# Attention side jobs of a transformer block, cut into two 64-row halves and put among the score tiles, with a new timetable

## The chip, the cores and the metric

The kernel runs on one core of a Trainium2 chip. The metric is the time of one execution on the device in microseconds (us), as the median of several runs; beside it stands one profiled execution, whose trace every row below comes from. The engines are named as in the profile: PE is TensorE's matmul, PEld its weight load, DVE is VectorE, ACT is ScalarE, POOL is GpSimd, SP is SyncE (SPq its queue of DMA issues).

## The reference

Input x is 8 batches of 1024 tokens of 256 numbers. Two stages follow, each with a layer norm before it, a layer norm on its result and the input added:

```
x = x + layernorm(attention(layernorm(x)))      # 16 heads of 16, softmax over 1024 keys, biases on q, k, v, out
x = x + layernorm(experts(layernorm(x)))        # 16 experts (8 chosen per token) and one shared, hidden size 128
```

Only the attention stage is touched by the change.

## The kernel before, in words

**Units.** In the attention stage a batch has 8 steps (four heads and one half of the 512 queries each), and a step has 8 units (one chunk of 128 keys each). So there are 64 units u in a batch and 512 in all. A unit works on four score tiles (128 keys x 512 queries, one per head). For each unit PE issues

- `st`: four score tiles (L535). A head's q and k lie in a 64-row stack, rows 0 to 63 or 64 to 127, so that a tile is a matmul with K=64, and two with different rows can run beside each other. ACT takes the exponential of each (L925) into `probs`. The tiles have three banks: tile n waits for the exponential of tile n-3.
- `smax`: four matmuls of the same size (L547), two steps ahead of the tiles, with queries and keys exchanged. DVE takes the row maxima of each (L1036). They too have three banks: the n-th waits until DVE has read the one three before it.
- `pv`: probs times v for the four heads (L557), eight matmul instructions of 128 rows x 32 columns. It waits for all four exponentials of its unit, and at the first unit of a step until ACT has copied `o_bank` away (L833, `o_stored`).
- in some units a part of a side job, all of them in one bank, `job_bank`.

In `batch` the order on PE in unit u is: two tiles of the next unit, one maximum matmul, pv, a maximum, a tile, a maximum, a tile, the job part, a maximum. So between one pv and the next there are four tiles and four maximum matmuls: at pv of unit u the tiles up to 4u+5 have been issued.

**Side jobs.** The table `JOBS` gives the unit of each: XT transposes the next batch's normed x (L573), QK (L581) and V (L590) project it, OP (L602) is the output projection of the batch before, SH (L594) transposes the row maxima of a step for its shift. A QK or V or OP job is six or twelve matmuls with K=128, cut into two parts for two units. A job's result is read at the start of the unit after its last part: `if u - 1 in JOBS`. DVE reads QK (L1057), XT (L1053) and SH (L1069) ahead of that unit's four maxima (at the first unit of a step `combine_maxima`, L1043, stands before both); QK and XT are first read by ACT, after the four exponentials of that unit; V and OP are read by ACT alone. The next job may not write `job_bank` before that (list `before`).

**The row for the shift.** The tiles of a step need the maxima of that step in row 32 of their stacks: SH, then DVE (L1069), then four DMAs of `load_shift` (L352). The first tile of a step waits for them (`shift_loaded`). All DMAs of the stage are issued by SP, in an order written out by hand. In its middle stand, for batch b:

```
gather(b, 3)
load_shift(b, 5)
...
if not last:
    load_stack(b + 1, 0, False)
gather(b, 4)
load_shift(b, 6)
```

`load_stack(b + 1, 0)` waits until DVE has read the fourth QK job of batch b + 1, then issues 14 DMAs (L339, L343). `gather` issues eight (L363, L364).

**Last batch.** From unit 50 on no maxima are left; the tiles have six banks (`late`), and all four tiles of the next unit are issued before pv.

Of the kernel before, what the change touches and what calls it, by code (L numbers as in the profile page):

```python
# [5 lines left out]
BATCHES, SEQ, D = 8, 1024, 256  # L6
HEADS = 16
DH = D // HEADS
CH = 128
# [7 lines left out]
RING = 3  # L17
VW = 2 * DH
EXPERTS, HID, TOPK = 16, 128, 8
ALL_E = EXPERTS + 1  # L20
# [25 lines left out]
for _kind, _off, _i, _at in (  # L46
# [3 lines left out]
    for _n, _u in enumerate(_at):  # L50
        JOBS[_u] = (_kind, _off, _i + _n // 2, _n % 2)

# [12 lines left out]
def skipped(job, first, last):  # L65
    kind, off, i, part = job
    return off == -1 and first or off == 1 and last or last and kind == "SH" and i == STEPS


# [7 lines left out]
def both_stages(nc, x, x1, wq, wk, wv, wo, biases, ob, ident_dram, out, comb_dram, gate_w, w_gate, w_up, w_down,  # L77
# [8 lines left out]
    with ctx:  # L86
# [126 lines left out]
        exp_done = sem("exp_done")  # L213
        pv_done = sem("pv_done")
        smax_ready = sem("smax_ready")
        smax_read = sem("smax_read")
# [302 lines left out]
        def _(pe):  # L519
            mm = nc.tensor.matmul  # L520
            before = []

            def st(U, s, kc, j, new_step):

                q, f, p, e, tile = s // 2, s % 2, j // 2, j % 2, 4 * U + j
                if new_step is not None:
                    pe.wait_ge(shift_loaded, 64 * (new_step + 1))
# [10 lines left out]
            def smax(S, s, kc, half, e):  # L538

                q, f = s // 2, s % 2  # L540
                p, c = kc // HC, kc % HC
                tok = f * HALF + c * CH
                n = 32 * S + 4 * kc + 2 * half + e
                if n >= RING:
                    pe.wait_ge(smax_read, n - RING + 1)
                rows = slice(64 * e, 64 * e + 64)
                mm(sm_bank[n % RING][:, :], q_stack[q][p][rows, tok:tok + CH],  # L547
                   k_stack[q][p][rows, half * HALF:(half + 1) * HALF], start=True, stop=True).then_inc(smax_ready, 1)

            def pv(U, S, s, kc):  # L550

                q = s // 2
                if kc == 0 and not (isinstance(S, int) and S == 0):
                    pe.wait_ge(o_stored, S)
                pe.wait_ge(exp_done, 4 * U + 4)
                for j in range(4):
                    last = mm(o_bank[32 * j:32 * j + 32, :], v_quad[q][:, kc, VW * j:VW * j + 32],  # L557
                              probs[0 if kc % 2 == 0 else 1][:, j, :], start=(kc == 0), stop=(kc == CHUNKS - 1))
                last.then_inc(pv_done, 1)


            def job(kind, B, i, part=None, job_bank=job_bank, banks=1, before=before):
# [41 lines left out]
                if part != 0:  # L604
                    last.then_inc(job_ready[kind], 1)


            READ = {"XT": "xT_read", "LG": "lg_read", "CB": "cbT_read", "GT": "gT_read"}
# [90 lines left out]
            for S in range(2):  # L699
                for n in range(4 * CHUNKS):  # L700
                    smax(S, S, n // 4, n // 2 % 2, n % 2)
# [5 lines left out]
            for j in range(RING):  # L707
                st(0, 0, 0, j, 0)

            def batch(b, first, last):  # L710
                for u in range(UNITS):
# [8 lines left out]

                    def maximum(half, e):
                        if maxima:
                            smax(S + 2, (s + 2) % STEPS, kc, half, e)

                    def scores(j):
                        if u + 1 < UNITS:
                            st(U + 1, (u + 1) // CHUNKS, (u + 1) % CHUNKS, j, S + 1 if kc == CHUNKS - 1 else None)
                        elif not last:
                            st(U + 1, 0, 0, j, S + 1)

                    if u == 0 and first:
                        st(U, s, kc, 3, None)
                    late = last and u >= 50
                    scores(0)
                    scores(1)
                    if late:
                        scores(2)
                        scores(3)
                    maximum(0, 0)
                    if last and u == UNITS - 1:  # L740
                        gu(0, 0, 0, True)
                    pv(U, S, s, kc)
                    maximum(0, 1)
                    if not late:
                        scores(2)
                    maximum(1, 0)
                    if not late:
                        scores(3)
# [42 lines left out]
        def _(act):  # L791
# [122 lines left out]
            def batch(b, first, last):  # L914
                for u in range(UNITS):
                    s, kc = u // CHUNKS, u % CHUNKS
                    U, S = UNITS * b + u, STEPS * b + s
                    for j in range(4):
# [4 lines left out]
                        if j == 0 and U >= 2:  # L923
                            act.wait_ge(pv_done, U - 1)
                        nc.scalar.activation(probs[kc % 2][:, j, :], bank_of(4 * U + j)[:, :],  # L925
                                             ACT.Exp).then_inc(exp_done, 1)
# [61 lines left out]
        def _(dve):  # L988
# [39 lines left out]

            def reduce(S, s, kc, half):

                f = s % 2
                p, c = kc // HC, kc % HC
                for e in range(2):
                    n = 32 * S + 4 * kc + 2 * half + e
                    dve.wait_ge(smax_ready, n + 1)
# [254 lines left out]
            for S in range(2):  # L1290
                for kc in range(CHUNKS):
                    reduce(S, S, kc, 0)
                    reduce(S, S, kc, 1)
                if S == 0:
                    combine_maxima(0, 0)
                    job("SH", 0, 0)

            def batch(b, first, last):
                for u in range(UNITS):
# [9 lines left out]
                    if maxima:  # L1309
                        reduce(S + 2, (s + 2) % STEPS, kc, 0)  # L1310
                    if u in SPLITS and not (first and SPLITS[u][0]):
# [15 lines left out]
                    if maxima:  # L1327
                        reduce(S + 2, (s + 2) % STEPS, kc, 1)
                    if not last and u in X_STATS:
# [263 lines left out]
```

## Time and profile before

| | us |
|---|---|
| median of 3 runs | 2856.01 (2855.09 to 2858.19) |
| the profiled execution's own time | 2851.14 |
| its span, first to last instruction | 2849.4 |
| PE busy | 2746.2 (96%) |
| DVE busy | 2233.9 (78%) |
| ACT busy | 1632.6 (57%) |
| mean granted TensorE clock | 0.989 of full speed |

The attention stage takes the first 57% of the span, the experts the rest. In the attention stage PE and DVE are both nearly full, in the expert stage only PE is. Busy shares of PE are no measure of how near it is to its peak, since a matmul's record begins when it is issued to the array and overlaps with the next one.

### The profile page before, as it was taken

To read this page: it belongs to the slowest core of one execution; us is meant where nothing else is said; L and a number is where in the kernel's file an instruction comes from. 1 tells how busy PE (TensorE), PEld (TensorE's weight loads), DVE (VectorE), ACT (ScalarE), POOL (GpSimd) and SP (SyncE) were. 2 spreads that over 40 slices of the span, in tenths; PEclk is the share of its full clock that TensorE was granted. 3 is DMA by queue.
4 is the path that set the end of the run, shared out by engine and by line. 5 is a ranking of instruction groups with operands and counts; after the bars stand their busy time and mean duration, and the time that the engine had idled before them with its cause. 6 is when DMAs were issued, how large, how long until landed. Compare 5 with 4: busy or idle time off the path is not lost.

```text
span 2849.4 us, 47584 instructions
## 1 busy us (share of the span) xinstructions
PE 2746.2 (96%) x16514; PEld 1685.8 (59%) x16514; DVE 2233.9 (78%) x4679; ACT 1632.6 (57%) x3095; POOL 954.7 (34%) x997
## 2 busy tenths in 40 slices
PE   5999999999999999999999999999999999999997
PEld 3434333343343343333433388888888888888886
DVE  4898998999999999999999667666666666666654
ACT  1477777777777777777778843333333333333332
POOL 4041462543533624625435545111111111111112
PEclk8899999999999999999999999999999999999999
DMA  5313422343234134333432323222222222232221
GB/s 88 55 27 57 65 60 54 57 85 57 56 63 64 42 65 64 64 56 59 69 64 72 88 78 105 82 79 77 73 82 83 79 79 71 83 82 79 79 74 54
DMA packets 136639, 197.32 MB, mean 69 GB/s; under 512 B 22336, under 2 KB 84816, under 8 KB 134352
## 3 DMA queue, kind: packets, MB, share of 16 engines
q1 hardware_dynamic: 136400, 194.29, 30.6%
q8 instruction: 131, 2.15, 0.3%
q14 instruction: 108, 0.88, 0.1%
HBM read 108.74 MB, written 17.30 MB: 44 GB/s over the span
## 4 chain that ended last, share of the span: by engine, by line
PE 82%; SPq 6%; DVE 5%; ACT 4%; issue 2%; POOL 1%; DMA 1%; POOLq 0%; ACTq 0%; DVEq 0%
PE o_bank L557 14%; PE y_bank L680 13%; PE g_bank L666 13%; PE u_bank L666 13%; PE sm_bank L547 12%; PE st_bank L535 7%; PE job_bank L581 4%; SPq L339 3%; DVE score_max L1036 3%; ACT probs L925 3%; PE job_bank L590 2%; PE job_bank L602 1%; SPq L352 1%; SPq L363 1%; SPq L364 1%
## 5 line engine op out<-in xcount | busy, mean ns | idle before, releaser
L1036 DVE TENSOR_REDUCE score_max<-sm_bank 128x1 f32<-128x512 f32 x2048 | 1302.3, 681 | 114.4 <-PE sm_bank L547 110.7
L925 ACT ACTIVATE probs<-st_bank 128x512 f32<-128x512 f32 x2023 | 1077.8, 601 | 319.0 <-PE st_bank L535 316.5
L547 PE MATMUL sm_bank<-qk_stack 64*128 64x512 f32 x2048 | 804.3, 465 | 18.7 <-DMA qk_stack<-qk_stack 10.5
L535 PE MATMUL st_bank<-qk_stack 64*128 64x512 f32 x2023 | 753.3, 453 | 30.1 <-ACT probs L925 24.5
L547 PEld LDWEIGHTS sm_bank<-qk_stack 64*128 64x128 f32 x2048 | 332.5, 187 | 581.6 <-DVE score_max L1036 537.9
L557 PE MATMUL o_bank<-probs,v_quad 128*32 128x512 f32 x4096 | 545.5, 605 | 9.1 <-ACT o_sb L833 7.0
L1193 DVE TENSOR_TENSOR h<-gate_act,u_bank 128x512 f32<-128x512 f32 x256 | 176.2, 688 | 312.9 <-ACT gate_act L887 312.9
L887 ACT ACTIVATE gate_act<-g_bank 128x512 f32<-128x512 f32 x272 | 162.4, 597 | 418.1 <-PE u_bank L666 418.0
L535 PEld LDWEIGHTS st_bank<-qk_stack 64*128 64x128 f32 x2023 | 313.7, 184 | 99.6 <-ACT probs L925 74.6
L898 ACT ACTIVATE h_hi<-h 128x512 fp32r<-128x512 f32 x272 | 172.2, 633 | 325.5 <-DVE h L1196 287.8
L680 PE MATMUL y_bank<-f_w_hi,h_hi 128*128 128x256 f32 x1088 | 311.7, 286 | 0.1
L680 PE MATMUL y_bank<-f_w_lo,h_hi 128*128 128x256 f32 x1088 | 307.6, 283 | 0.0
L680 PE MATMUL y_bank<-f_w_hi,h_lo 128*128 128x256 f32 x1088 | 307.6, 283 | 0.0
L1473 POOL TENSOR_SCALAR f_x_in<-f_x_in,f_mv,f_rstd 128x256 f32<-128x256 f32 x64 | 90.3, 1419 | 624.8 <-DVE f_rstd L1107 624.8
L1437 POOL TENSOR_TENSOR recip_tmp<-sum_part,recip 128x512 f32<-128x512 f32 x96 | 123.7, 1289 | 466.6 <-DVE recip L1077 461.6
L1204 DVE TENSOR_TENSOR h_lo<-h,h_hi 128x512 fp32r<-128x512 f32 x272 | 189.4, 696 | 47.2 <-ACT h_hi L898 43.6
L666 PE MATMUL g_bank<-f_xT_hi,f_w_hi 128*128 128x512 f32 x544 | 215.4, 396 | 0.5 <-DVE h L1193 0.5
L666 PE MATMUL g_bank<-f_xT_lo,f_w_hi 128*128 128x512 f32 x544 | 215.0, 395 | 0.0
L680 PEld LDWEIGHTS y_bank<-f_w_hi,h_hi 128*128 128x128 f32 x1088 | 207.5, 191 | 8.6 <-DVE h_lo L1204 0.3
L680 PEld LDWEIGHTS y_bank<-f_w_hi,h_lo 128*128 128x128 f32 x1088 | 207.8, 191 | 8.0
L666 PE MATMUL u_bank<-f_xT_hi,f_w_lo 128*128 128x512 f32 x544 | 211.9, 389 | 0.0
L666 PE MATMUL g_bank<-f_xT_hi,f_w_lo 128*128 128x512 f32 x544 | 211.6, 389 | 0.0
(200 smaller groups left out, 3874.5 us busy)
## 6 DMA issues: line engine op xcount, KB each, us to landing
cb<-comb_dram SPq DMA_DIRECT2D x256, 256.0 KB, 3.6
qk_stack<-qk_parts SPq DMA_DIRECT2D x360, 128.0 KB
x_in<-in_x SPq DMA_DIRECT2D x8, 1024.0 KB, 6.6
o_part<-o_sb SPq DMA_DIRECT2D x256, 32.0 KB, 2.0
sum_part<-o_sb SPq DMA_DIRECT2D x256, 32.0 KB, 2.0
x_res<-in_x SPq DMA_DIRECT2D x16, 512.0 KB, 3.9
x<-x_res SPq DMA_DIRECT2D x16, 512.0 KB, 3.1
f_x_in<-x SPq DMA_DIRECT2D x16, 512.0 KB, 3.9
```

The source lines that it names most:

```text
L535: mm(bank_of(tile)[:, :], k_stack[q][p][rows, kc * CH:(kc + 1) * CH], q_stack[q][p][rows, f * HALF:(f + 1) * HALF], start=True, stop=True) ...
L547: mm(sm_bank[n % RING][:, :], q_stack[q][p][rows, tok:tok + CH], k_stack[q][p][rows, half * HALF:(half + 1) * HALF], start=True, stop=True ...
L557: last = mm(o_bank[32 * j:32 * j + 32, :], v_quad[q][:, kc, VW * j:VW * j + 32], probs[0 if kc % 2 == 0 else 1][:, j, :], start=(kc == 0), ...
L666: last = mm(bank[:, :], w_exp[b][:, e, col + k * HID:col + (k + 1) * HID], fxT[par][a][:, k, :], start=(t == 0), stop=(t == len(steps) - 1))
L680: last = mm(y_bank[:, c, :], h[i][a][:, c * CH:(c + 1) * CH], w_exp[b][:, e, 2 * D:3 * D], start=(e == 0 and t == 0 and c % 2 == 0), stop= ...
L887: a_(gate_act[i][:, :], g_bank[i][:, :], ACT.Silu).then_inc(E["silu_done"], 1)
L898: a_(h[i][0][:, :], h32[i][:, :], ACT.Copy).then_inc(E["h_hi_done"], 1)
L925: nc.scalar.activation(probs[kc % 2][:, j, :], bank_of(4 * U + j)[:, :], ACT.Exp).then_inc(exp_done, 1)
L1036: v.reduce_max(score_max[f][:, HC * (2 * p + e) + c, half:half + 1], sm_bank[n % RING][:, :], AX_X).then_inc(smax_read, 1)
L1193: v.tensor_tensor(h32[i][:, :], gate_act[i][:, :], u_bank[i][:, :], ALU.mult).then_inc(E["gated_done"], 1)
L1204: v.tensor_tensor(h[i][1][:, :], h32[i][:, :], h[i][0][:, :].bitcast(F32), ALU.subtract).then_inc(E["h_ready"], 1)
L1437: g.tensor_tensor(recip_tmp[:, :], sum_part[f][:, :], recip[:, :], ALU.mult).then_inc(recip_chain, 1)
```

## The change

- XT, QK, V and OP jobs are issued by a new function `job_rows`: their K=128 matmuls become two halves with K=64 (rows 0 to 63 first, then rows 64 to 127), each half in three thirds. A unit's job part is thus six pieces. They stand between the tiles and the maximum matmuls, each next to one of the other rows. The second half waits for the first (`job_rows_done`), and so does the second part for the first part.
- In every unit pv now comes first, then tile 4u+6, a maximum, tile 4u+7, two maxima, tile 4u+8, a maximum, tile 4u+9. In a unit with a job part the first piece stands ahead of tile 4u+6 and the second ahead of the first maximum.
- The heads are taken in the order 0, 2, 1, 3 (`HEAD_AT`), and the maxima in an order of rows that depends on whether the unit has a job (`MAX_AT`).
- New timetable: XT at units 22, 24, 26, 28 (before 23, 24, 27, 28); QK at 30, 33, 36, 39 and 52, 55, 58, 61, each with the unit after it (before 29, 31, 35, 37 and 51, 53, 55, 59); V at 42, 44, 47, 50 (before 39, 43, 45, 47); SH at 32 in place of 33, else as before; OP as before.
- The special order of the last batch's units from 50 on is gone (the six banks are still there). Six tiles are issued ahead of the first unit instead of three.

```diff
-JOBS = {
-    23: ("XT", 1, 0, None), 24: ("XT", 1, 1, None), 27: ("XT", 1, 2, None), 28: ("XT", 1, 3, None),
-}
-for _s in range(STEPS):
-    JOBS[8 * _s + 1] = ("SH", 0, _s + 1, None)
+JOBS = {}
+for _i, _u in enumerate((1, 9, 17, 25, 32, 41, 49, 57)):
+    JOBS[_u] = ("SH", 0, _i + 1, None)
+for _i, _u in enumerate((22, 24, 26, 28)):
+    JOBS[_u] = ("XT", 1, _i, None)
 for _kind, _off, _i, _at in (
-        ("OP", -1, 0, (5, 6, 7, 8)), ("OP", -1, 2, (15, 16, 20, 21)),
-        ("QK", 1, 0, (29, 30, 31, 32, 35, 36, 37, 38)), ("V", 1, 0, (39, 40, 43, 44, 45, 46, 47, 48)),
-        ("QK", 1, 4, (51, 52, 53, 54, 55, 56, 59, 60))):
+        ("OP", -1, 0, (5, 7)), ("OP", -1, 2, (15, 20)), ("QK", 1, 0, (30, 33, 36, 39)),
+        ("V", 1, 0, (42, 44, 47, 50)), ("QK", 1, 4, (52, 55, 58, 61))):
...
+            def job_rows(job, b, e, third):
...
+                rows = slice(64 * e, 64 * e + 64)
+                if third == 0:
+                    if e == 1 or part == 1:
+                        pe.wait_ge(job_rows_done, rows_done[0])
+                    if e == 0 and part != 1:
+                        if before:
+                            pe.wait_ge(*before.pop(0))
...
+                elif kind == "QK":
+                    m, half, n = i // 4, i // 2 % 2, "qk"[i % 2]
+                    a, w = PARTS[third]
+                    last = mm(job_bank[:, :], w_parts[n][w][rows, part, m * 128:(m + 1) * 128],
+                              xT[a][rows, part, half * HALF:(half + 1) * HALF],
+                              start=(part == 0 and third == 0 and e == 0), stop=(part == 1 and third == 2 and e == 1))
+                else:
...
+                    for k in range(KD):
+                        last = mm(job_bank[:, part * D:(part + 1) * D], left[a][rows, k, c * CH:(c + 1) * CH],
+                                  right[w][rows, k, :], start=(e == 0 and third == 0 and k == 0),
+                                  stop=(e == 1 and third == 2 and k == KD - 1))
...
                     pv(U, S, s, kc)
-                    maximum(0, 1)
-                    if not late:
-                        scores(2)
-                    maximum(1, 0)
-                    if not late:
-                        scores(3)
-                    if u in JOBS and not skipped(JOBS[u], first, last):
-                        kind, off, i, part = JOBS[u]
-                        job(kind, b + off, i, part)
-                    maximum(1, 1)
+                    if with_job:
+
+                        job_rows(JOBS[u], b, 0, 0)
+                        st(4 * U + 6)
+                        job_rows(JOBS[u], b, 0, 1)
+                        maximum(0)
+                        job_rows(JOBS[u], b, 0, 2)
+                        st(4 * U + 7)
+                        maximum(1)
+                        maximum(2)
+                        st(4 * U + 8)
+                        job_rows(JOBS[u], b, 1, 0)
+                        maximum(3)
+                        job_rows(JOBS[u], b, 1, 1)
+                        st(4 * U + 9)
+                        job_rows(JOBS[u], b, 1, 2)
+                    else:
+                        st(4 * U + 6)
+                        maximum(0)
+                        st(4 * U + 7)
+                        maximum(1)
+                        maximum(2)
+                        st(4 * U + 8)
+                        if u in JOBS and not skipped(JOBS[u], first, last):
+                            job("SH", b, JOBS[u][2])
+                        maximum(3)
+                        st(4 * U + 9)
```

## Rows read from the trace of the kernel before

**Rows 1.** Six whole batches in one window: length, busy and count per engine, clock, DMA

```profile
294.74:1463.13 1168.39, 1140.52 (x7152) 460.00 (x7152) 1091.51 (x1999) 914.08 (x1729) 521.12 (x613) 1.00 0.34 60
```

**Rows 2.** Timeline of PE, a unit without a job: start, us, line, matmul, count

```profile
740.81 1.06 PE L557 MATMUL o_bank<-probs,v_quad 128*32 128x512 f32 x8
741.81 0.49 PE L547 MATMUL sm_bank<-qk_stack 64*128 64x512 f32 x1
...
742.15 0.62 PE L547 MATMUL sm_bank<-qk_stack 64*128 64x512 f32 x2
742.39 0.39 PE L535 MATMUL st_bank<-qk_stack 64*128 64x512 f32 x1
...
743.09 0.50 PE L547 MATMUL sm_bank<-qk_stack 64*128 64x512 f32 x1
743.51 1.07 PE L557 MATMUL o_bank<-probs,v_quad 128*32 128x512 f32 x8
```

**Rows 3.** Timeline of DVE and of ACT in the same unit

```profile
742.34 2.48 DVE L1036 TENSOR_REDUCE score_max<-sm_bank 128x1 f32<-128x512 f32 x4 [0.22 <-PE sm_bank L547]
...
742.37 2.06 ACT L925 ACTIVATE probs<-st_bank 128x512 f32<-128x512 f32 x4 [0.90 <-PE st_bank L535]
```

**Rows 4.** Timeline of PE, a unit with a QK job part

```profile
792.23 1.06 PE L557 MATMUL o_bank<-probs,v_quad 128*32 128x512 f32 x8
793.22 0.49 PE L547 MATMUL sm_bank<-qk_stack 64*128 64x512 f32 x1
...
793.88 0.50 PE L581 MATMUL job_bank<-xT_hi,wq_hi 128*128 128x512 f32 x1
794.22 0.40 PE L581 MATMUL job_bank<-xT_lo,wq_hi 128*128 128x512 f32 x1
...
794.77 0.49 PE L547 MATMUL sm_bank<-qk_stack 64*128 64x512 f32 x1
...
795.44 0.64 PE L557 MATMUL o_bank<-probs,v_quad 128*32 128x512 f32 x4
```

**Rows 5.** Timeline of PE, the V job part of another unit

```profile
822.21 0.28 PE L590 MATMUL job_bank<-wv_hi,xT_lo 128*128 128x256 f32 x1
822.33 0.28 PE L590 MATMUL job_bank<-wv_lo,xT_hi 128*128 128x256 f32 x1
```

**Rows 6.** Timeline of PE, first and last pv record of a unit with an XT job

```profile
755.90 1.07 PE L557 MATMUL o_bank<-probs,v_quad 128*32 128x512 f32 x8 [0.21 <-ACT o_sb L833]
...
758.82 0.64 PE L557 MATMUL o_bank<-probs,v_quad 128*32 128x512 f32 x4
```

**Rows 7.** Timeline, PE and DVE: unit 33, which reads a QK job and has SH

```profile
783.33 1.06 PE L557 MATMUL o_bank<-probs,v_quad 128*32 128x512 f32 x8
...
786.30 0.64 PE L557 MATMUL o_bank<-probs,v_quad 128*32 128x512 f32 x4
...
783.90 0.72 DVE L1057 SCALAR_TENSOR_TENSOR qk_parts<-job_bank,bias,qk_parts 128x512 fp32r<-128x512 f32 x1
784.53 2.47 DVE L1036 TENSOR_REDUCE score_max<-sm_bank 128x1 f32<-128x512 f32 x4
786.92 0.27 DVE L1069 TENSOR_SCALAR shift_row<-job_bank 16x128 fp32r<-16x128 f32 x1
```

**Rows 8.** Timeline of SP's queue, units 39 to 45, and PE's first tile of step 6

```profile
803.18 10.90 SPq L339 DMA_DIRECT2D qk_stack<-qk_parts  x12
...
820.62 2.53 SPq L352 DMA_DIRECT2D qk_stack<-shift_row  x4
...
826.12 0.72 PE L535 MATMUL st_bank<-qk_stack 64*128 64x512 f32 x2
```

**Rows 9.** Timeline of SP's queue and of PE in unit 14

```profile
724.41 2.54 SPq L352 DMA_DIRECT2D qk_stack<-shift_row  x4
...
728.03 0.56 PE L535 MATMUL st_bank<-qk_stack 64*128 64x512 f32 x2 [1.06 <-DMA qk_stack<-shift_row]
```

**Rows 10.** Timeline of PE, a late unit (57) of the last batch

```profile
1628.51 1.06 PE L557 MATMUL o_bank<-probs,v_quad 128*32 128x512 f32 x8 [0.36 <-ACT probs L925]
...
1630.47 1.06 PE L557 MATMUL o_bank<-probs,v_quad 128*32 128x512 f32 x8 [0.23 <-ACT probs L925]
```

More of the change, by code:

```diff
@@ L18 @@
 VW = 2 * DH
+HEAD_AT = (0, 2, 1, 3)
+MAX_AT = {True: ((0, 1), (0, 0), (1, 1), (1, 0)), False: ((0, 0), (1, 0), (0, 1), (1, 1))}
 EXPERTS, HID, TOPK = 16, 128, 8
@@ L36 @@
 PARTS = [(0, 0), (1, 0), (0, 1)]
-JOBS = {
-    23: ("XT", 1, 0, None), 24: ("XT", 1, 1, None), 27: ("XT", 1, 2, None), 28: ("XT", 1, 3, None),
-}
-for _s in range(STEPS):
-    JOBS[8 * _s + 1] = ("SH", 0, _s + 1, None)
+JOBS = {}
[3 more added lines that the diff above has]
+    JOBS[_u] = ("XT", 1, _i, None)
 for _kind, _off, _i, _at in (
[3 rows of a table removed]
+        ("OP", -1, 0, (5, 7)), ("OP", -1, 2, (15, 20)), ("QK", 1, 0, (30, 33, 36, 39)),
+        ("V", 1, 0, (42, 44, 47, 50)), ("QK", 1, 4, (52, 55, 58, 61))):
     for _n, _u in enumerate(_at):
-        JOBS[_u] = (_kind, _off, _i + _n // 2, _n % 2)
+        for _part in range(2):
+            JOBS[_u + _part] = (_kind, _off, _i + _n, _part)
 X_STATS = {0: 0, 2: 1, 5: 2, 6: 3, 7: 4, 8: 5, 9: 6, 10: 7}
@@ L67, in skipped, with among_scores @@
     return off == -1 and first or off == 1 and last or last and kind == "SH" and i == STEPS
+def among_scores(u, first, last):
+    return u in JOBS and JOBS[u][0] != "SH" and not skipped(JOBS[u], first, last)
 def wait_apart(engine, semaphore, value, passed):
@@ L521, in _, with st @@
             before = []
[L523 to L527, printed above, removed]
+            def st(tile):
+                U, i = tile // 4, tile % 4
+                if U >= UNITS * BATCHES:
+                    return
+                S, kc, j = U // CHUNKS, U % CHUNKS, HEAD_AT[i]
+                s = S % STEPS
+                q, f, p, e = s // 2, s % 2, j // 2, j % 2
+                if kc == 0 and i == 0:
+                    pe.wait_ge(shift_loaded, 64 * (S + 1))
                 if tile >= LATE + 6:
@@ L536, in st, with smax @@
                    q_stack[q][p][rows, f * HALF:(f + 1) * HALF], start=True, stop=True).then_inc(st_ready, 1)
-            def smax(S, s, kc, half, e):
+            def smax(S, s, kc, i, with_job):
                 q, f = s // 2, s % 2
                 p, c = kc // HC, kc % HC
+                half, e = MAX_AT[with_job][i]
                 tok = f * HALF + c * CH
-                n = 32 * S + 4 * kc + 2 * half + e
+                n = 32 * S + 4 * kc + i
                 if n >= RING:
@@ L552, in pv @@
                 q = s // 2
-                if kc == 0 and not (isinstance(S, int) and S == 0):
+                if kc == 0 and S > 0:
                     pe.wait_ge(o_stored, S)
@@ L706, in _ @@
             before.pop(0)
-            for j in range(RING):
-                st(0, 0, 0, j, 0)
+            for tile in range(6):
+                st(tile)
             def batch(b, first, last):
@@ L719, in batch, with maximum @@
                         pe.wait_ge(v_copied, QUADS * b + s // 2 + 1)
-                    def maximum(half, e):
+                    with_job = among_scores(u, first, last)
+                    def maximum(i):
                         if maxima:
[L723 to L736, printed above, removed]
-                        scores(2)
-                        scores(3)
-                    maximum(0, 0)
+                            smax(S + 2, (s + 2) % STEPS, kc, i, with_job)
                     if last and u == UNITS - 1:
@@ L1027, in seed_a, with reduce @@
                 seed(seed_no(f"a{f}", B), var_a[f][:, :], mv_a[f][:, :, 1], rstd_a[f][:, :])
-            def reduce(S, s, kc, half):
+            def reduce(S, s, kc, pair, with_job):
                 f = s % 2
                 p, c = kc // HC, kc % HC
-                for e in range(2):
-                    n = 32 * S + 4 * kc + 2 * half + e
+                for i in (2 * pair, 2 * pair + 1):
+                    half, e = MAX_AT[with_job][i]
+                    n = 32 * S + 4 * kc + i
                     dve.wait_ge(smax_ready, n + 1)
@@ L1291, in _ @@
                 for kc in range(CHUNKS):
-                    reduce(S, S, kc, 0)
-                    reduce(S, S, kc, 1)
+                    reduce(S, S, kc, 0, False)
+                    reduce(S, S, kc, 1, False)
                 if S == 0:
@@ L1309, in batch @@
                     if maxima:
-                        reduce(S + 2, (s + 2) % STEPS, kc, 0)
+                        reduce(S + 2, (s + 2) % STEPS, kc, 0, among_scores(u, first, last))
                     if u in SPLITS and not (first and SPLITS[u][0]):
@@ L1327, in batch @@
                     if maxima:
-                        reduce(S + 2, (s + 2) % STEPS, kc, 1)
+                        reduce(S + 2, (s + 2) % STEPS, kc, 1, among_scores(u, first, last))
                     if not last and u in X_STATS:
```

34 lines of the change are left out of this document (30 added, 4 removed).

## The prediction

> **What bounds the kernel now.** I read the window over six whole batches first. It gives 1168.39/6 = 194.73 us a batch, 3.04 a unit, with PE 98% and DVE 93% busy at the full clock [rows 1]. The clock has nothing to give, so the question is what ends a unit. That is read from the timelines, as the distance from one pv to the next.
>
> A unit without a job takes 2.70 us [rows 2]. Its PE steps are: pv to the first pair of score matmuls 1.00, first to second pair 0.34, second to third 0.24. The reader should see that the fourth maximum matmul comes only at 743.09, behind a gap. It waits for the first of the four reduces, which began 0.53 after its matmul and takes about 0.68 (2.48 for four, 0.60 apart) [rows 3]: 742.34 + 0.68 + 0.06 = 743.08. ACT gives the same end: 742.37, one exponential later (the four take 2.06, so about 0.49 apart) and 0.60 long, is 743.46, and pv starts at 743.51. So 2.70 is a round trip PE to DVE or ACT and back; neither engine is full. Since the second matmul of a pair starts with the first, I call both by one time.
>
> A unit with a QK part takes 3.21 [rows 4]. Here PE sets the end: 0.99, then 0.66 to the job, 0.34 and 0.24 between its matmuls, 0.31 back to 64 rows, 0.67 to pv. Each change of tiling costs: 0.31 to 0.34 where 0.24 is the step inside one. That is the 36 units of 64 which the change attacks.
>
> **The change part by part.** All times from here are after the start of the unit's pv.
>
> *A QK unit.* Seven pairs stand in one tiling: job and tile 6, job and maximum 0, job and tile 7, maxima 1 and 2, tile 8 and job, maximum 3 and job, tile 9 and job. By PE's steps they start at 1.00, 1.34, 1.58, 1.82, 2.06, 2.30, 2.54, and pv follows 0.33 later: 2.87. The columns streamed are the same as before; two changes of tiling are saved. But maximum 0 is now in the second pair, at 1.34 and not at 1.00, and all four maxima lie behind the pv. DVE can start at 1.34 + 0.43 = 1.77 (a matmul whose load is hidden lasts 0.39, not 0.50), ends at 2.45, and maximum 3, in the same one of three banks, goes at 2.51 instead of 2.30. Its weight load carries the wait, so the next of its rows follows after 0.34: 2.85, and pv at 3.18. I take 3.17 against 3.21: 16 units a batch, -0.6. The low end is PE's own 2.87, the high one 3.37, if every pair takes 0.34.
>
> The step of 0.24 inside 64 rows is seen once per plain unit [rows 2]. The Trainium skill, TensorE: Matmul & The Clock Gate, Part 3, The mechanism, says that a weight load overlaps with a running matmul only when the row group differs. In a run of pairs that use both row groups each load would then stand open, 0.34 a pair; the trace has 742.15 to 742.39 with the same two row groups in both pairs, so here it does not agree. By the rule a QK unit is 3.37, by the row 3.17.
>
> *V and OP units.* Each piece is two matmuls of 256 columns, 0.12 apart [rows 5]. Matmuls start in order, so tile 6 and maximum 0 come 0.12 later: 3.29. Against about 3.21 that is +0.08: V 8 x 0.08 = +0.6 a batch. OP counts only at 15, 16, 20, 21, because unit 14 waits for DMAs anyway (below): 4 x 0.08 = +0.3.
>
> *XT units.* They took 2.92 [rows 6]: four short transposes. In the new order maximum 0 stands behind three of them (at about 1.40) and the same round trip gives 3.23: 4 x 0.31 = +1.2.
>
> *The units that read a job.* QK and XT are read by DVE ahead of the four maxima of the next unit, 0.63 from its start to the next reduce [rows 7]. Before, this mostly fell into a job unit, where DVE had slack; four times it fell into a plain unit, and unit 33 took 2.97 [rows 7]. Now all twelve reads fall into plain units. After a QK unit DVE is free at 1.77 + 4 x 0.60 - 3.17 = 1.00, reads until 1.63, and maximum 0 is reduced from 1.63, not 1.53: +0.10 each, +1.2, with 0.2 for unit 32, which has `combine_maxima` too, less four times 0.2 before: +0.6.
>
> *SH next to a job.* The first piece of a job now stands right behind pv, and it waits until `job_bank` has been read. The timetable puts a job directly behind SH five times: units 26, 33, 42, 50, 58; before there was always a unit between. SH is read by DVE after all four reduces of the unit before: the last one lets go at 744.73, which is 1.22 after pv [rows 3], the read takes 0.27 [rows 7], so the job starts at 1.55, not 1.00. Tile 6, and behind it ACT, and all of PE wait with it: 4 x 0.55. In unit 33 it is worse: unit 32 has combine (0.17), the QK read and a norm's statistics on DVE, and SH is read at 2.0, +1.0. Sum +3.2. Below: 0, if the read slipped into an earlier gap, which DVE's order excludes.
>
> *SP's queue.* This is the largest term. The fourth QK job moves from units 37, 38 to 39, 40. `load_stack` of the next batch waits for its read, and it stands ahead of `gather` 4 and `load_shift` 6, which the first tile of step 6 needs. From the first stack DMA to the last shift DMA it is 803.18 to 822.6, and from there to a tile that waits for it 1.65 (726.4 to 728.03 [rows 9]): 21.1 us at least [rows 8], up to 22.5 in other batches, 21.8 in the mean. The tile came at 826.12, so the slack was about 2 here and 1.1 in the mean. In the new order the DMAs can start at 1.75 in unit 41, and the tile is due at 1.58 in unit 46: 2.80 + 3.84 + 3 x 3.29 - 1.75 + 1.58 = 16.3. PE waits 21.8 - 16.3 = 5.5; of this 0.8 comes back because the exponentials for the next pv are done meanwhile: +4.7 a batch. Late next: `load_stack` 1, `gather` 5 and `load_shift` 7 behind it, 22 us more, against 25 to their tile, so nothing. Between 3 and 6 is my bound.
>
> Unit 14 is already such a wait: PE idles 1.06 before the tile [rows 9]. What is lost or won in units 0 to 13 of a batch is therefore mostly hidden, OP at 5 to 8 among it.
>
> *The last batch.* Without the special order tiles 6 and 7 of a unit come behind the pv again, and a late unit is a round trip of 2.70 and not 1.96 [rows 10]. Some ten units of 1.96 to 2.25 lose 0.6 each, about 1 comes back where the shift of step 7 is late anyway: +5. With the six early tiles, +0.
>
> *Nothing for* the head order and `MAX_AT`: pairs of opposite rows formed before too, and a plain unit keeps its round trip through ACT. The expert stage is the same.
>
> **Sum.** XT, QK and V for the next batch run in seven batches: 7 x (-0.6 + 0.6 + 1.2 + 0.6 + 3.2 + 4.7) = 68. OP 7 x 0.3 = 2, last batch 5: 75. The profiled execution's own time of 2851.1 becomes 2926. The median of the runs lies 4.9 above that execution, so I predict 2931, 2.6% slower.
>
> **The rivals.**
>
> *A, SP's queue is not late* (its DMAs go out faster when PE is slower to use them). For: 1.1 us of slack was there. Against: the chain is fixed issue time, 0.6 to 0.7 a DMA. Then 7 x 4.7 = 33 less: 2898.
>
> *B, the other side: the pieces cost PE nothing.* They would fill the time in which PE waits for DVE and ACT, and a job unit would be a plain one, 2.70: 252 job units x 0.47 = 118 less, of which some 30 go again to unit 14 and to a longer wait in 46: 2843, 0.4% faster. For: the gap ahead of 743.09 in a plain unit. Against: seven pairs at 0.24 make 2.87. It decides from about 2.76 a job unit downwards; maximum 0 would have to be free of its place in the second pair.
>
> *C, open weight loads:* seven pairs at 0.34, 0.20 more in 252 units, 50 us: 2981. The skill's rule above is this case. For: the step after every change of tiling is 0.34. Against: the 0.24 of the third pair.
>
> *D, a piece and its tile don't run beside each other.* Two more slots of 0.24 a unit at least, 0.5 x 252 = 126: 3057. For: the trace has no job in 64 rows. Against: tile and maximum matmul of the same shape do.
>
> **How the numbers follow.** Chances: the forecast 0.60 (its own range 2900 to 2960), A 0.13, B 0.10, C 0.10, D 0.07. The range from 2862 to 2980 leaves out B nearly whole, D, and the upper part of C, some 2 in 10. A change within 0.2% is about what a measurement of this kernel can't tell from none. Faster by more comes only from B: 0.09. Within 0.2%: 0.04, out of B and the edge of A. Slower: 0.87.
>
> **What would show it.** In the profile after: QK units at 3.17, V and OP 3.29, XT 3.23; step 0.24 between pairs inside a job unit; the fourth maximum matmul waiting for DVE in them. In the waits: PE for the shift's DMAs some 5 us in each of seven batches, at the first tile of step 6; PE's job matmuls waiting for L1069 five times a batch. A batch of about 205 us. The expert stage unchanged. I would be wrong if job units fell under 2.9, or if the tile of step 6 found its shift there.

## The result, and the profile after

| | before | after |
|---|---|---|
| median | 2857.1 us (2855.09 to 2859.19) | 2957.17 us (2953.89 to 2960.86) |
| span of the profiled execution | 2849.4 | 2954.3 |
| mean granted TensorE clock | 0.989 | 0.977 |

The ratio is 1.0352, 95% interval 1.034 to 1.0365: slower by 100 us, where 75 were forecast. The profiled executions took 2851.1 and 2956.1, 105 apart: that of the kernel before lies 6 under its median. The sums over units below are of these two.

The window over six whole batches, to be read against [rows 1] (length, then busy and count of PE, PEld, DVE, ACT, POOL, clock, DMA):

```profile
306.57:1553.34 1246.77, 1155.83 (x8112) 541.70 (x8113) 1082.41 (x2000) 907.96 (x1729) 524.73 (x613) 0.98 0.32 57
```

A batch takes 207.8 us, 13.1 more. PE is 93% busy where it was 98%, at a clock of 0.98 where it was 1.00. DVE and ACT do the same number of instructions in no more time (1082 and 908 us against 1092 and 914); PE has 960 more matmuls, halves of former ones, and is busy for 15 of the 78 us that six batches grew by. The other 63 are idle time of PE.

A unit with a QK part (unit 36), PE's timeline, against [rows 4]:

```profile
833.74 1.07 PE L573 MATMUL o_bank<-probs,v_quad 128*32 128x512 f32 x8
834.73 0.49 PE L657 MATMUL job_bank<-xT_hi,wq_hi 64*128 64x512 f32 x1
834.74 0.49 PE L550 MATMUL st_bank<-qk_stack 64*128 64x512 f32 x1
...
835.07 0.39 PE L563 MATMUL sm_bank<-qk_stack 64*128 64x512 f32 x1
835.29 0.39 PE L550 MATMUL st_bank<-qk_stack 64*128 64x512 f32 x1
...
835.52 0.40 PE L563 MATMUL sm_bank<-qk_stack 64*128 64x512 f32 x2
835.75 0.49 PE L657 MATMUL job_bank<-xT_hi,wq_hi 64*128 64x512 f32 x1
...
836.25 0.49 PE L563 MATMUL sm_bank<-qk_stack 64*128 64x512 f32 x1
...
836.58 0.39 PE L550 MATMUL st_bank<-qk_stack 64*128 64x512 f32 x1
...
836.91 0.64 PE L573 MATMUL o_bank<-probs,v_quad 128*32 128x512 f32 x4
```

The reader is to see job piece and tile starting together, steps of 0.22 to 0.24 between pairs inside the tiling, and one gap of 0.50 ahead of the fourth maximum matmul at 836.25. The unit takes 3.17, as forecast, against 3.21.

Unit 33, the job directly behind SH; PE's timeline:

```profile
823.57 1.07 PE L573 MATMUL o_bank<-probs,v_quad 128*32 128x512 f32 x8
825.52 0.50 PE L657 MATMUL job_bank<-xT_hi,wk_hi 64*128 64x512 f32 x1 [0.88 <-DVE shift_row L1141]
...
827.72 0.64 PE L573 MATMUL o_bank<-probs,v_quad 128*32 128x512 f32 x4
```

The first piece comes 1.95 after pv, not 1.00, and the unit takes 4.14.

SP's queue and PE in units 41 to 47 of the same batch, against [rows 8]; under it the window table of units 46, 47 and 48:

```profile
851.60 10.78 SPq L349 DMA_DIRECT2D qk_stack<-qk_parts  x12
...
869.52 2.54 SPq L362 DMA_DIRECT2D qk_stack<-shift_row  x4
...
873.14 0.79 PE L550 MATMUL st_bank<-qk_stack 64*128 64x512 f32 x1 [4.53 <-DMA qk_stack<-shift_row]
```

```profile
865.99:874.29 8.30, 3.38 (x19) 1.14 (x17) 4.00 (x7) 3.48 (x7) 0.00 (x0) 0.87 0.27 81
874.29:879.24 4.95, 4.95 (x30) 3.15 (x29) 2.07 (x4) 2.73 (x6) 0.00 (x0) 0.53 1.13 153
879.24:882.44 3.20, 3.20 (x31) 1.99 (x29) 2.50 (x6) 1.79 (x4) 0.00 (x0) 1.00 0.85 128
```

PE stands for 4.5 us, and then something the forecast did not have: the next unit, in which PE is never idle, takes 4.95 where its like takes 3.19. Its granted clock is 0.53, near the lower level of 1.2 GHz; one unit later it is 1.00 again.

Mean length of units over six batches, in us, from the distances between pv starts in the two traces (a table worked out, not a view; for XT the units before, then those after):

```
                              before  after           before  after
plain (0, 2, 13, 19)           2.70    2.74   unit 46    3.23    8.58
QK (30, 36, 37 ...)            3.22    3.18   unit 47    3.23    4.94
V (43, 44, 45 ...)             3.23    3.19   unit 26    2.71    3.65
XT (24, 27; 22, 24, 28)        2.91    3.17   unit 33    2.96    4.13
last batch, all               179.4   194.2   42, 50, 58 2.71    3.75, 3.64, 3.64
```

### The profile page after: what moved, and what is told of

Its sections match the earlier page's. It is cut to its first block, busy times and chain, and to the rows that moved or that the text cites. A ratio compares the mean times of both kernels' runs of the same rounds, so it can differ in the third digit from the quotient of the medians.

```text
span 2954.3 us, 49634 instructions
## 1 busy us (share of the span) xinstructions
PE 2766.5 (94%) x17634; PEld 1779.3 (60%) x17634; DVE 2222.5 (75%) x4679; ACT 1626.9 (55%) x3095; POOL 959.1 (32%) x997
## 4 chain that ended last, share of the span: by engine, by line
PE 66%; DVE 15%; SPq 11%; issue 4%; ACT 2%; DMA 1%; POOL 1%; POOLq 0%; ACTq 0%; DVEq 0%
PE y_bank L747 13%; PE g_bank L733 12%; PE u_bank L733 12%; DVE score_max L1108 12%; PE o_bank L573 10%; SPq L349 7%; PE sm_bank L563 6%; PE st_bank L550 5%; PE job_bank L657 3%; PE job_bank L665 2%; ACT probs L996 1%; SPq L362 1%; SPq L374 1%; SPq L353 1%; SPq L373 1%
## 5 line engine op out<-in xcount | busy, mean ns | idle before, releaser
L1108 DVE TENSOR_REDUCE score_max<-sm_bank 128x1 f32<-128x512 f32 x2048 | 1282.9, 680 | 221.5 <-PE sm_bank L563 216.7
L550 PE MATMUL st_bank<-qk_stack 64*128 64x512 f32 x2023 | 847.0, 451 | 42.7 <-DMA qk_stack<-shift_row 39.2
L563 PE MATMUL sm_bank<-qk_stack 64*128 64x512 f32 x2048 | 754.7, 456 | 61.9 <-DVE score_max L1108 43.4
L573 PE MATMUL o_bank<-probs,v_quad 128*32 128x512 f32 x4096 | 555.5, 615 | 20.7 <-ACT o_sb L904 11.6
L550 PEld LDWEIGHTS st_bank<-qk_stack 64*128 64x128 f32 x2023 | 363.2, 187 | 307.3 <-ACT probs L996 140.9
L563 PEld LDWEIGHTS sm_bank<-qk_stack 64*128 64x128 f32 x2048 | 344.9, 190 | 245.8 <-DVE score_max L1108 214.8
```

The source lines that it names most:

```text
L1108: v.reduce_max(score_max[f][:, HC * (2 * p + e) + c, half:half + 1], sm_bank[n % RING][:, :], AX_X).then_inc(smax_read, 1)
```

## The experiments

Every kernel here does the whole computation and leaves nothing out. "Before", run again beside them, had medians of 2854.4 to 2855.9; the ratios go by the one beside each. The changed kernel itself stands at 2957.17, ratio 1.0352.

**1. SP's order.** The changed kernel, with

```diff
-                if not last:
-                    load_stack(b + 1, 0, False)
                 gather(b, 4)
                 load_shift(b, 6)
+                if not last:
+                    load_stack(b + 1, 0, False)
```

> The changed kernel with one edit on SP: the stack load of the next batch is issued after gather 4 and the shift load of step 6, not before. Theory (SP's order makes the wait at unit 46, and the wait makes TensorE's clock fall in unit 47): units 46 and 47 go from 8.6 and 4.9 us to 2.74 and 3.19, a batch from 207.8 to about 200.2, the clock stays full, and the time falls by 7 x 7.6 = 53 us to about 2904. Rival (the issue time is only moved): the stack is then late for the first maximum of unit 48 or the shift of step 7 for unit 54, and at least half of the 7.6 us comes back there. Rival (the clock in 47 falls for another reason, such as the traffic of the stack's DMAs): 47 stays at 4.9, 12 us less gained.

Measured: 2907.62, ratio to before 1.0183 (1.0167 to 1.02). Units 46 and 47, the window table:

```profile
845.25:848.60 3.35, 2.95 (x18) 1.03 (x17) 2.65 (x5) 3.21 (x7) 0.00 (x0) 1.00 0.95 122
848.60:851.99 3.39, 3.27 (x30) 2.03 (x30) 3.26 (x6) 2.77 (x6) 0.00 (x0) 1.00 0.91 206
```

2904 was expected. A batch is 200.9, 6.9 less. The order of the DMAs was the wait, and with the wait gone the clock holds, although the stack's DMAs still run in these units (DMA share 0.95 and 0.91): the rival by which their traffic slows unit 47 falls. Unit 46 is 3.35 and not 2.74: there ACT reads the V job and makes a split, 1.25 us in all, ahead of the exponentials, and PE waits for an exponential:

```profile
847.14 0.49 PE L550 MATMUL st_bank<-qk_stack 64*128 64x512 f32 x1 [0.40 <-ACT probs L996]
```

**2. The table alone.** The kernel before, with nothing but the new `JOBS` (its code still puts a whole job between two maximum matmuls):

```diff
...
+for _i, _u in enumerate((1, 9, 17, 25, 32, 41, 49, 57)):
...
+for _i, _u in enumerate((22, 24, 26, 28)):
...
-        ("OP", -1, 0, (5, 6, 7, 8)), ("OP", -1, 2, (15, 16, 20, 21)),
-        ("QK", 1, 0, (29, 30, 31, 32, 35, 36, 37, 38)), ("V", 1, 0, (39, 40, 43, 44, 45, 46, 47, 48)),
-        ("QK", 1, 4, (51, 52, 53, 54, 55, 56, 59, 60))):
+        ("OP", -1, 0, (5, 7)), ("OP", -1, 2, (15, 20)), ("QK", 1, 0, (30, 33, 36, 39)),
+        ("V", 1, 0, (42, 44, 47, 50)), ("QK", 1, 4, (52, 55, 58, 61))):
...
```

> The kernel before with nothing but the new JOBS table: K=128 jobs, its own order on PE, its late order. Theory (the table alone makes SP late): the tile of step 6 is due in unit 46 at 16.1 us after the stack's DMAs can start, which need 21.8; with the lower clock after it some 7 us a batch, about 1 more for reads in plain units, none for SH since a job stands at the end of its unit: 2857 + 7 x 8 = 2913. Rival (the 64-row pieces and the order on PE cause most of it): under 2875.

Measured: 2915.83, ratio 1.0213 (1.019 to 1.0236). The same wait stands in the old code. Waits of one unit 46 (who waited for whom: us, times, longest), and units 46 and 47:

```profile
PEld st_bank L535 <- DMA qk_stack<-shift_row: 6.2, 1, 6.2
```

```profile
851.96:860.84 8.88, 3.10 (x18) 1.18 (x17) 3.71 (x6) 2.96 (x7) 0.00 (x0) 0.80 0.24 73
860.84:865.56 4.72, 4.72 (x24) 1.91 (x23) 2.11 (x4) 2.44 (x6) 0.00 (x0) 0.65 1.11 154
```

**3. The ring of three.** The changed kernel, in units with a job:

```diff
                         job_rows(JOBS[u], b, 0, 0)
-                        st(4 * U + 6)
-                        job_rows(JOBS[u], b, 0, 1)
                         maximum(0)
+                        job_rows(JOBS[u], b, 0, 1)
+                        st(4 * U + 6)
                         job_rows(JOBS[u], b, 0, 2)
```

> The changed kernel with maximum 0 and tile 4u+6 exchanged in units with a job, so that the maximum stands in the first pair. Theory (the ring of three maximum banks sets such a unit's 3.18): DVE starts 0.33 earlier, maximum 3 goes at 2.27 instead of 2.51, and the unit ends at 2.94, where the exponentials of tiles 6 and 7 come last: -0.24 in QK, V and XT units, some of it lost to units 14 and 46, so about 6 us a batch and 42 us in all: about 2914. Rival (PE's own steps or the pieces set the 3.18): no change, 2957. Rival (the tile put later costs as much as the maximum gains): within 10 us of 2957.

Measured: 2937.91, ratio 1.0289 (1.027 to 1.0309). The unit did what was expected: PE's timeline has pv at 826.63, the maximum at 1.00 after it, the fourth at 828.93 and the next pv at 829.59, 2.96 in all. The total gave 19 of the 43 us. The rest went to units 14 and 15, which grew from 3.30 and 3.38 to 4.87 and 4.50 (the DMAs of step 2 keep their time), in four batches of six with a low clock behind the wait, and to 46 (8.58 to 9.58). Unit 36, then units 14 and 15:

```profile
826.63 1.06 PE L573 MATMUL o_bank<-probs,v_quad 128*32 128x512 f32 x8
...
827.63 0.50 PE L563 MATMUL sm_bank<-qk_stack 64*128 64x512 f32 x1
...
828.93 0.49 PE L563 MATMUL sm_bank<-qk_stack 64*128 64x512 f32 x1
...
829.59 0.64 PE L573 MATMUL o_bank<-probs,v_quad 128*32 128x512 f32 x4
```

```profile
756.73:761.54 4.81, 2.61 (x18) 0.94 (x17) 3.60 (x8) 2.06 (x5) 0.00 (x0) 1.00 0.04 11
761.54:766.09 4.55, 4.46 (x30) 2.99 (x30) 2.38 (x6) 2.80 (x6) 0.00 (x0) 0.62 0.00 0
```

Here no DMA moved anything in unit 15 (last three columns: clock 0.62, DMA share 0.00, 0 GB/s), so the low clock follows PE's idle time, not traffic.

**4. The read of SH.** The changed kernel, on DVE (not in the last batch):

```diff
-                        if part != 0:
+                        if part != 0 and (kind != "SH" or last):
                             job(kind, b + off, i)
...
+                    if u in JOBS and JOBS[u][0] == "SH" and not last:
+                        job("SH", b, JOBS[u][2])
                     if maxima:
                         reduce(S + 2, (s + 2) % STEPS, kc, 1, among_scores(u, first, last))
```

> The changed kernel with DVE reading SH in its own unit, ahead of the last two maxima, instead of at the start of the next unit (not in the last batch). Theory (a job right behind SH waits for that read): units 26, 33, 42, 50 and 58 fall from 3.65, 4.13, 3.75, 3.64, 3.64 to 3.18; what 42 gives is lost at 46 where SP is late: 2.4 us a batch, 17 in all, about 2940. Rival (these units are long because of the transposes' or the read job's own place): they stay, and the read costs up to 0.2 in each SH unit: 2957 to 2970.

Measured: 2937.39, ratio 1.028 (1.026 to 1.0299). Units 26, 33, 42, 50, 58 became 3.18, 3.20, 3.19, 3.19, 3.17, together 2.9 a batch; unit 46 took 0.5 of it back (9.09), and unit 14 gave 0.5 (2.81).

**5. The late order.** Two tiles ahead of pv again from unit 50 of the last batch on:

```diff
+                    late = last and u >= 50
+                    if late:
+                        st(4 * U + 6)
+                        st(4 * U + 7)
...
                     else:
-                        st(4 * U + 6)
+                        if not late:
+                            st(4 * U + 6)
                         maximum(0)
-                        st(4 * U + 7)
+                        if not late:
+                            st(4 * U + 7)
```

> The changed kernel with the special order of the last batch's units from 50 on put back (two tiles ahead of pv). Theory (the round trip pv, tile, two exponentials, pv sets these units): units 51 to 61 go from 2.66 to about 2.05 as before, -0.6 in ten units: 5 to 6 us less, about 2951. Rival (the clock or the late shift sets the last batch's end): within 2 us of 2957.

Measured: 2952.92, ratio 1.0344 (1.033 to 1.0358). That is 4 less than the changed kernel, and the intervals of the two overlap, so the total alone decides little. In the trace six of the eleven units from 51 to 61 take 1.66 to 2.17 where most took 2.66, but units 49 and 50 grew from 4.07 and 3.83 to 4.98 and 5.20, both at a clock of 0.50 (see 10).

**6. Whole jobs, first try.** The six `job_rows` lines go out, and the job stands in one piece:

```diff
                         maximum(1)
+                        kind, off, i, part = JOBS[u]
+                        job(kind, b + off, i, part)
                         maximum(2)
```

> The changed kernel with its timetable and its order of tiles and maxima, but each job part issued whole with K=128 between the second and the third maximum. Theory (the two halves save 0.04 us a unit at their place and cost the wait for SH right behind pv): job units take 3.22, units 26, 33, 42, 50, 58 no more than that, the waits at 46 and 14 stay, so 2.9 less and 36 x 0.03 more a batch: about 2943, with up to 10 less where DVE's slack is used. Rival (the halves are worth the two changes of tiling, 0.35 a unit): 2957 + 252 x 0.35 - 20 = 3025.

Measured: 3034.35, ratio 1.063 (1.0616 to 1.0645), a miss by 91. The rival's 3025 is near, but by luck: its reason, that the halves save two changes of tiling worth 0.35 a unit, does not hold in number 8, where a whole job costs 0.04 a unit more. A job unit took 3.67. I had left the row order `MAX_AT` of the units with pieces: without the pieces between them three matmuls of rows 64 to 127 follow each other, and behind the job three of rows 0 to 63, and two more slots of 0.24 appear. Number 8 tests that.

**7. The table of before,** with the rest of the change: the diff of number 2 the other way round, on the changed kernel.

> The changed kernel with the JOBS table of before. Theory (the table is what makes SP late, but the first piece right behind pv needs the gaps of the new one): the wait at 46 shrinks from 5 to under 1, and in its place seven jobs a batch (units 24, 28, 31, 37, 39, 53, 55) stand directly behind a job that DVE reads, 0.7 us each: a batch of about 200, in all about 2905. Rival (the order on PE costs by itself what the table costs): 2950 or more. Rival (the table alone is the loss): under 2875.

Measured: 2931.85, ratio 1.0269 (1.0255 to 1.0283). The wait at 46 is gone as expected, but the jobs behind a job that DVE reads wait 1.0 us each and not 0.7, and they are eight, not seven (I had missed unit 29): 8.0 a batch against 4.9, so the total is 27 over the 2905 expected. PE in unit 31:

```profile
807.12 1.06 PE L573 MATMUL o_bank<-probs,v_quad 128*32 128x512 f32 x8
809.29 0.50 PE L657 MATMUL job_bank<-xT_hi,wk_hi 64*128 64x512 f32 x1 [1.11 <-DVE qk_parts L1129]
```

**8. Whole jobs, with rows in pairs.** Number 6, and the row order of a unit without pieces, on PE and in the reads on DVE:

```diff
-                            smax(S + 2, (s + 2) % STEPS, kc, i, with_job)
+                            smax(S + 2, (s + 2) % STEPS, kc, i, False)
...
-                        reduce(S + 2, (s + 2) % STEPS, kc, 0, among_scores(u, first, last))
+                        reduce(S + 2, (s + 2) % STEPS, kc, 0, False)
...
-                        reduce(S + 2, (s + 2) % STEPS, kc, 1, among_scores(u, first, last))
+                        reduce(S + 2, (s + 2) % STEPS, kc, 1, False)
```

> As e6_whole_jobs, but with the row order of the units without a job in all units, so that tiles and maxima stand in pairs of opposite rows. Theory (e6's 3.67 us were two more slots of 0.24 because three matmuls of one row group followed each other; a whole job at its own place takes 3.22): job units 3.22, XT 2.92, no wait behind SH at 26, 33, 42, 50, 58, waits at 14 and 46 as in the changed kernel: 2.4 us a batch less than it, about 2940. Rival (whole jobs between the maxima cost 3.67 whatever the rows): 3034 again.

Measured: 2936.81, ratio 1.029 (1.0276 to 1.0304). Job units 3.22, XT 2.91. So number 6 cost what it did by its rows, and at the place where the change puts them the 64-row halves lose 18 to 20 us against whole jobs. That is the wait behind SH: with it taken out (number 4, 2937.39) halves and whole jobs come out equal in the total.

**9. Before, with the new table and experiment 1's order:** the diffs of numbers 2 and 1, both on the kernel before.

> The kernel before with the new JOBS table and the SP order of e1_queue. Theory (SP's queue and the clock behind its wait are all that the table costs): against e2_timetable_alone units 46 to 48 lose 9 us a batch, which leaves about 196 a batch: 2866. Rival (the table costs something of its own, by DVE's reads in plain units): 2875 or more. Rival (the table is better once SP is out of the way): under 2852.

Measured: 2869.48, ratio 1.0053 (1.0039 to 1.0067). A batch is 196.3: of the table's loss of 61 us (number 2) 46 were SP's wait and the clock behind it.

**10. All repairs together.** The diffs of numbers 1, 3, 4 and 5, and one that takes 14 DMAs out of the way of unit 14:

```diff
-                    load_stack(b, 3, False)
                 for s in range(3):
...
                     load_shift(b, s + 2)
+                    if s == 0 and not first:
+                        load_stack(b, 3, False)
```

> The changed kernel with all repairs: maximum 0 in the first pair of a job unit, SH read in its own unit, the stack load of the next batch behind shift 6, the load of stack 3 behind shift 2, the late order of the last batch. Theory (each term is a wait of its own and they add): job units 2.95, no wait at 14, 26, 33, 42, 46, 50, 58, full clock: a batch of about 191.4 against 194.7 before, last batch under 179: about 2832, 0.8% faster than the kernel before. Rival (the time goes to a new wait, for DVE in the units that read a job or for SP's queue at steps 3 and 7): 2850 to 2870.

Measured: 2846.76, ratio 0.9971 (0.9962 to 0.998): faster than before by 0.3%, not by the 0.8% expected. A batch is 192.6, 1.2 more than expected. Against number 1 five units are 0.22 to 0.25 longer each, 15, 31, 39, 47 and 55, at whose end pv waits for the copy of `o_bank`, and unit 54 is 0.49 longer, because the first tile of step 7 now waits for its shift's DMAs: a part of the rival came true. The last batch is 187.0, more than before's 179.4. The wait at the first tile of step 7, then the last batch's units 47 to 50, window table:

```profile
842.89 0.50 PE L551 MATMUL st_bank<-qk_stack 64*128 64x512 f32 x1 [0.45 <-DMA qk_stack<-shift_row]
```

```profile
1587.20:1591.92 4.72, 3.14 (x19) 1.14 (x18) 4.72 (x10) 2.44 (x5) 4.72 (x4) 1.00 0.03 7
1591.92:1595.23 3.31, 3.05 (x14) 0.95 (x13) 1.46 (x2) 2.54 (x6) 1.34 (x1) 0.62 0.21 50
1595.23:1600.21 4.98, 4.98 (x16) 1.57 (x16) 1.34 (x8) 2.99 (x7) 0.00 (x0) 0.50 0.05 13
1600.21:1605.42 5.21, 5.21 (x18) 1.92 (x17) 1.23 (x6) 1.81 (x5) 0.00 (x0) 0.50 0.45 129
```

**11. The same with whole jobs:** number 10 with the diffs of numbers 6 and 8 in place of number 3's.

> As e10_best, but each job part whole with K=128 behind the second maximum, and the row order of plain units. Theory (once the ring of maximum banks is out of the way the 64-row halves are worth 3.22 - 2.95 = 0.27 in a job unit of QK, V and OP, less where pv waits for the copy of o_bank, and nothing in XT): about 6.5 us a batch more than e10_best: 2847 + 48 = 2895. Rival (the halves give nothing, the other repairs do it): within 10 us of 2847.

Measured: 2868.53, ratio 1.0051 (1.0037 to 1.0064). So the halves are worth 0.8%, 22 to 23 us, once nothing else binds; I had expected 48. A job unit is 2.95 against 3.22, but the units behind pieces keep new waits: against this kernel 15, 31, 39, 47 and 55 lose 0.2 to 0.3, units 41, 54 and 60 together 0.9, and unit 46 alone 0.6 (3.36 against 2.74).

**12. The router's transposes two units earlier.** In the last batch PE waits in unit 47 for DVE to read the first of them.

```diff
-                        if u in (45, 47):
-                            gate_transposed((u - 45) // 2)
+                        if u in (43, 45):
+                            gate_transposed((u - 43) // 2)
```

and the same shift of their reads on ACT and DVE.

> As e10_best, with the two transposes of the router's weights and their reads two units earlier in the last batch (units 43 to 47 instead of 45 to 49), so that PE doesn't wait for DVE in unit 47. Theory (after that wait TensorE's clock falls to half in units 48 to 50, which take 13.5 us and not some 8): 4 to 6 us less, about 2842, and the clock of these units is full. Rival (the clock falls there for the little work of PE in the late units): within 2 us of 2847.

Measured: 2840.61, ratio 0.9955 (0.9941 to 0.9968), 0.45% faster than before; the best of all. The same units of the last batch, each shorter than in number 10:

```profile
1588.94:1592.19 3.25, 3.06 (x19) 1.01 (x17) 3.25 (x6) 2.58 (x6) 3.25 (x3) 1.00 0.00 0
1592.19:1594.86 2.67, 2.22 (x15) 0.64 (x13) 1.52 (x5) 1.97 (x5) 1.20 (x1) 1.00 0.15 35
1594.86:1598.18 3.32, 3.08 (x15) 1.01 (x15) 1.18 (x7) 2.72 (x6) 0.00 (x0) 1.00 0.21 51
1598.18:1601.08 2.90, 2.90 (x17) 1.16 (x16) 0.98 (x6) 1.80 (x5) 0.00 (x0) 1.00 0.06 17
```

Units 48 to 50 take 8.9 at the full clock, 13.5 in number 10. Part of the wait only moved (unit 45 went from 2.90 to 4.34), and there the clock did not fall. All five runs of this kernel (2840.1 to 2843.5) lie under all eleven of number 10 (2845.5 to 2851.8). But the wait in unit 47 does not bring the low clock every time. The kernel before has it too, and so has number 11 (4.69, then a clock of 1.00 in units 48 to 50), while in number 9, with the order of before, the same wait was followed by a clock of 0.50 to 0.71. Before, units 47, 48 and 49:

```profile
1601.06:1605.93 4.87, 3.29 (x19) 1.17 (x17) 4.87 (x9) 2.76 (x6) 4.87 (x4) 1.00 0.02 5
1605.93:1608.60 2.67, 2.22 (x15) 0.71 (x13) 1.02 (x2) 2.23 (x5) 0.91 (x1) 1.00 0.23 55
1608.60:1611.69 3.09, 3.04 (x17) 0.98 (x16) 1.17 (x7) 2.49 (x6) 0.00 (x0) 1.00 0.14 35
```

## Why the prediction was right, step by step

**Direction and mechanism were right; the sum was 25 us short.** 75 was forecast, 100 measured. In the two traces it is 13 a batch in seven batches and 15 in the last, 106 in all, against 10.0 and 5. Some errors cancelled: V, OP and XT were put 1.4 a batch too high, SP's queue 2.2 too low.

**QK units, right.** 3.17 forecast, 3.17 to 3.18 measured, with maximum 3 gone late because its bank was read late. Experiment 3 moved just that and got 2.96 against 2.94. The step of 0.24 (0.22 to 0.24 in the rows) holds along a whole run of pairs, so rival C (open weight loads) is refused here: 3.37 would have been read. The Trainium skill, TensorE: Matmul & The Clock Gate, Part 3, The mechanism, has a load overlap only with another row group; these rows don't agree with it. Rival D fell with the same rows. Rival B too; even with the ring out of the way the unit stays at 2.95.

**V, OP and XT, too high by 0.10, 0.10 and 0.06.** 3.29 was forecast, 3.19 measured. I let tile 6 wait for both small matmuls issued ahead of it; the trace starts it with the first (last section).

**Readers of a job, about right:** 2.76 to 2.85 for seven of the twelve where 2.80 was forecast, more where DVE has other work there too (41: 3.29, behind a norm's three small operations; 60: 3.15, behind a reciprocal), and in units 23, 57 and 63. With that, with plain units at 2.74 and not 2.70, which I had put at nothing, and with longer units at 8, 15, 31 and 63, all terms but SH and SP's queue cost 3.3 a batch (13.1 less 2.9 less 6.9) instead of 2.1. Experiment 9 gives 1.6 of it to the table; the rest, 1.7, is what is left for the order on PE, by difference.

**SH next to a job, right:** +3.2 forecast, 2.9 measured (experiment 4).

**SP's queue, mechanism right, size too small: this is the mis-sized term.** 4.7 forecast, 6.9 measured (experiment 1). Unit 46 is 5.8 longer than a plain unit, not 5.5 less 0.8. The waiting tile starts 7.4 after pv in the mean, where 1.58 + 5.5 = 7.1 was forecast. The next pv comes 1.15 behind it in each of the six batches, so nothing came back; that stretch already runs at a clock of 0.50 (873.14 to 874.29), while in unit 14, at the full clock, pv comes 0.66 behind such a tile. And the clock is still low in the next unit, another 1.6 to 1.8 a batch. "The clock has nothing to give" was read from the kernel before; it had something to lose. Of the inputs, the chain's length was right (21.8 in the mean of six batches), though the twelve stack DMAs in it are 0.9 apart and not 0.6 to 0.7, as rival A has it; the start was off: 2.2 into unit 41, not 1.75, because DVE reads the QK job behind a norm's operations and two reduces. Rival A (the queue is not late) is refused by experiments 1 and 2.

**The last batch, the other mis-sized term:** 5 forecast, 14.8 measured, from one trace of each kernel. The late units gave 6.0, as forecast before what was to come back. The wait at 14 was longer and unit 15 ran at clock 0.50, 3.4 together; units 48 to 50 gave another 3.4 at a clock of 0.50 to 0.59; 2.0 are spread over other units. Number 12 shows that the low clock in 48 to 50 can hang on the wait in unit 47. That the change brought it is not shown: the kernel before has the same wait, and its clock held in the one execution that was traced, which is near the fast end of its runs (2851.1; thirty others took 2850.7 to 2862.4). The medians, 100 apart and not 105, would fit a clock that often falls there before the change as well.

**Left open.** Why a plain unit takes 0.04 more in the new order was not tried; nor was what decides whether the clock falls behind a wait like that in unit 47.

## What to carry to other kernels

Where DMAs are issued in a fixed order by hand, a job that moves two units later moves everything that stands behind its wait in the queue: count the issue times from its new place to the next thing that is due, each kind of DMA by its own. A piece put right behind a long matmul group takes over every wait for its bank, so a free slot on the engine is not enough; the reader must have been there. And price a wait of several microseconds on TensorE by the units that follow it too, since its clock may fall.

## What the runs showed of the hardware that I had not expected

- TensorE's granted clock fell to its lower level, 1.2 GHz, behind PE waits: 0.53 in unit 47 after 4.5 us of idle time, 0.62 after the wait in unit 14 of experiment 3, 0.50 in units 49 and 50 of the last batch of number 10. There it stayed low over two whole units in which PE's records are gapless (4.98 of 4.98, 5.21 of 5.21). Unit 47 took 4.95 where an equal unit took 3.19. Idle times of 1.6 us in unit 47 of the last batch were followed by the low clock in numbers 9 and 10 and by the full one in the kernel before and number 11.
- Matmuls of different row groups do not start strictly in the order of issue. In a V unit two job matmuls of 256 columns on rows 0 to 63 are issued ahead of a tile on rows 64 to 127; the tile starts with the first of them, 0.22 ahead of the second:

```profile
860.60 0.38 PE L665 MATMUL job_bank<-wv_hi,xT_hi 64*128 64x256 f32 x1
860.60 0.50 PE L550 MATMUL st_bank<-qk_stack 64*128 64x512 f32 x1
860.82 0.28 PE L665 MATMUL job_bank<-wv_hi,xT_hi 64*128 64x256 f32 x1
```

  The Trainium skill, TensorE: Matmul & The Clock Gate, Part 3, The mechanism, has matmuls in strict order of issue in start and end; these starts don't agree with it.
- Three matmuls of one row group in a row cost a slot each, 0.24, where two of opposite rows share one: 3.67 against 3.22 a unit (experiments 6 and 8).
